# A token loop of graph layers on one core: layer 0 at both ends of the tensor phase, pair-0 results of layer 1 in evicted banks, new engine orders, one pair halved once

## The chip, the cores and the metric

One core of a Trainium2 chip runs the whole kernel. The metric is the time of one execution on the device in microseconds (us).

## What is computed

The reference has three parts. The first, the tokeniser, is the one that the change touches: for each of 64 × 64 frames (V = 75 nodes, 3 channels) it applies three graph layers and averages over the nodes.

```python
def _layer(x, A, W, b, g, be, m, v, relu):
    x = jnp.einsum('btvc,co->btvo', x, W)
    x = jnp.einsum('uv,btvo->btuo', A, x)
    x = x + b
    x = (x - m) * (g * jax.lax.rsqrt(v + EPS)) + be
    if relu:
        x = jax.nn.relu(x)
    return x
x = _layer(x, A, W0, b0, g0, be0, m0, v0, relu=True)     # 3 -> 128
x = _layer(x, A, W1, b1, g1, be1, m1, v1, relu=True)     # 128 -> 128
x = _layer(x, A, W2, b2, g2, be2, m2, v2, relu=False)    # 128 -> 64
return x.mean(axis=2)
```

The tokens are then joined with a text input, go through one attention layer and through 30 feed-forward steps (tanh, sigmoid gate, layer norm, 64 × 64 product). Those parts are the same in both kernels.

## The kernel before

`setup` folds the norms into the weights, splits weights into an fp16 high and an fp16 low part, and stores the input, already mixed by A once, in DRAM rows. `tokenise` (L478) is the token loop. `fuse` does the third layer's product, attention and feed-forward.

`tokenise` goes over GROUPS = 205 bodies. One body handles four sets of five frames; the sets are numbered in pairs, pair 0 and pair 1 (the argument p). A set has 5 × 75 = 375 columns. The stages of one pair are:

- layer 0 (`layer0`, L552, matmul L563): six matmuls of 64 rows into the PSUM banks 0 and 1. All pairs share these two banks.
- high and low parts of its ReLU: ScalarE writes the fp16 high part of bank 0, the f32 value of bank 0 and the fp16 high part of bank 1 (`y0_high`, L624 to L626). GpSimd makes the low part of the first (`y0_low`, L649), VectorE that of the second, straight from bank 1 (`y0_low`, L682). When L625 and L682 are done, the banks are free.
- mixing with A (`mix`, L567, matmul L580): 36 matmuls, two row halves side by side, into banks 2 and 3 for pair 0 and 4 and 5 for pair 1, one bank for each set of the pair.
- ScalarE takes the mixed result out of PSUM: fp16 high of the first set (`z1_high`, L630), f32 of the second (L631). VectorE makes the fp16 low part of the first (`z1_low`, L687).
- layer 1 (`layer1`, L586): three fp16 matmuls (L593 to L595) for the first set into bank 6, one f32 matmul (L599, two instructions) for the second into bank 7, for either pair.
- weighing (`weigh`, L693) on VectorE: ReLU against the bias and product with the column means of A, from bank 6 or 7 into `y1`. After that bank is free.
- pooling: GpSimd adds the nodes 0 to 36 onto 37 to 73 (`halve`, L658), then 37 to 55 onto 56 to 74 (L660), so that 19 numbers are left for a frame; VectorE sums these for both pairs at once (`pool_nodes`, L700), two bodies later.

All tiles between the stages exist twice (`par`), PSUM banks do not.

The order of the work is written out by hand, one list for each engine (`body` in each block), and kept together by counting semaphores: an engine waits until another's counter has reached a value. `y0_unit` and `pair_unit` turn body and pair into counts; in layer 0 pair 1 comes before pair 0, everywhere else pair 0 first. `steps` (L514) runs three bodies, a loop whose turn holds two bodies, and two last bodies. TensorE's body is: layer 0 of pair 1 of the next body, mixing of pair 0 and of pair 1, layer 0 of pair 0 of the next body, layer 1 of pair 1 of the body before, layer 1 of pair 0 of this one. SyncE fetches the input of the body after next once this body's layer 0 has been counted twice.

Of the kernel before, what the change touches and what calls it, by code (L numbers as in the profile page):

```python
# [36 lines left out]
GF = 5  # L37
# [440 lines left out]
def tokenise(nc, ps, zs, zst, z_stored, zst_loaded, pooledT, AThi, ATlo, abar, W0K, W1hi, W1lo, W1s, negb1):  # L478

    with ExitStack() as ctx:  # L480
# [29 lines left out]
        Y0B, Z1B, Y1B = 0, 2, 6  # L510
# [17 lines left out]
        def y0_unit(it, p):  # L528

            return it * PAIRS + 1 - p  # L530

        def pair_unit(it, p):

            return it * PAIRS + p

        with nc.Block() as block:
# [14 lines left out]
            def _(pe):  # L551
                def layer0(it, par, p, loads):  # L552

                    n = y0_unit(it, p)
                    if late(n, 1):
                        pe.wait_ge(y0f_done, n)
                        pe.wait_ge(y0lo_by_dve, n)
                    pe.wait_ge(zst_loaded[par], loads * (2 * 16))
                    for t in range(CHUNKS // 2):
                        for half in range(2):  # L560
                            rows = slice(HALF * half, HALF * half + HALF)
                            c0 = p * HC + t * C
                            last = nc.tensor.matmul(ps[:, Y0B + half, t * C:(t + 1) * C], zst[rows, par, c0:c0 + C],  # L563
                                                    W0K[rows, :], start=True, stop=True, skip_group_check=True)
                    last.then_inc(y0_ready, 1)

                def mix(it, par, p):  # L567

                    n = pair_unit(it, p)
                    pe.wait_ge(y0lo_by_pool, y0_unit(it, p) + 1)  # L570
                    pe.wait_ge(y0lo_by_dve, y0_unit(it, p) + 1)
                    if late(n, 2):
                        pe.wait_ge(z1lo_done, n - 1)
                        pe.wait_ge(z1f_done, n - 1)
                    for t in range(CHUNKS):
                        f0, w = SPAN[t]
                        for y, a in ((y0hi, AThi), (y0hi, ATlo), (y0lo, AThi)):
                            for j in range(2):
                                rows = slice(HALF * j, HALF * j + HALF)
                                last = nc.tensor.matmul(ps[:, Z1B + 2 * p + j, f0 * V:f0 * V + w],  # L580
                                                        y[rows, par, p, t * C:(t + 1) * C], a[rows, BAND0[t]:BAND0[t] + w],
                                                        start=(t == 0 and y is y0hi and a is AThi),
                                                        stop=(t == CHUNKS - 1 and y is y0lo), skip_group_check=True)
                    last.then_inc(z1_ready, 1)

                def layer1(it, par, p):  # L586

                    n = pair_unit(it, p)
                    pe.wait_ge(z1lo_done, n + 1)
                    if late(n, 1):  # L590
                        pe.wait_ge(y1_done[0], n)
                    o = ps[:, Y1B, 0:GV]
                    nc.tensor.matmul(o, W1hi[:], z1hi[:, par, p, :], start=True, stop=False)  # L593
                    nc.tensor.matmul(o, W1hi[:], z1lo[:, par, p, :], start=False, stop=False)
                    nc.tensor.matmul(o, W1lo[:], z1hi[:, par, p, :], start=False, stop=True).then_inc(y1_ready[0], 1)  # L595
                    pe.wait_ge(z1f_done, n + 1)
                    if late(n, 1):
                        pe.wait_ge(y1_done[1], n)
                    nc.tensor.matmul(ps[:, Y1B + 1, 0:GV], W1s[:], z1f[:, par, p, :], start=True, stop=True).then_inc(y1_ready[1], 1)  # L599

                layer0(0, 0, 1, 1)
                layer0(0, 0, 0, 1)

                def body(it, par, pair, last=False):

                    if not last:
                        layer0(it + 1, 1 - par, 1, pair + 2)
                    mix(it, par, 0)
                    mix(it, par, 1)
                    if not last:  # L610
                        layer0(it + 1, 1 - par, 0, pair + 2)
# [7 lines left out]
            def _(act):  # L619
                def y0_high(it, par, p):  # L620
                    act.wait_ge(y0_ready, y0_unit(it, p) + 1)
                    if late(it, 1):
                        act.wait_ge(y0lo_by_pool, y0_unit(it, p) - 1)
# [4 lines left out]
                def z1_high(it, par, p):  # L628
                    act.wait_ge(z1_ready, pair_unit(it, p) + 1)
                    nc.scalar.activation(z1hi[:, par, p, :], ps[:, Z1B + 2 * p, 0:GV], ACT.Identity).then_inc(z1hi_done, 1)  # L630
                    nc.scalar.activation(z1f[:, par, p, :], ps[:, Z1B + 2 * p + 1, 0:GV], ACT.Identity).then_inc(z1f_done, 1)  # L631

                y0_high(0, 0, 1)
                y0_high(0, 0, 0)

                def body(it, par, pair, last=False):
                    if not last:
                        y0_high(it + 1, 1 - par, 1)
                    z1_high(it, par, 0)
                    if not last:  # L640
                        y0_high(it + 1, 1 - par, 0)
                    z1_high(it, par, 1)
# [3 lines left out]
            def _(pool):  # L646
                def y0_low(it, par, p):
                    pool.wait_ge(y0f_done, y0_unit(it, p) + 1)
# [3 lines left out]
                def halve(it, par, p):  # L652

                    n = pair_unit(it, p)
# [4 lines left out]
                    pool.wait_ge(halved, n + 1)  # L659
                    nc.gpsimd.tensor_tensor(y[:, :, U2:V], y[:, :, U2:V], y[:, :, U1:U2], ALU.add).then_inc(quartered, 1)  # L660

                y0_low(0, 0, 1)
                y0_low(0, 0, 0)

                def body(it, par, pair, last=False):
                    if not last:
                        y0_low(it + 1, 1 - par, 1)
                    if late(it, 1):
                        halve(it - 1, 1 - par, 0)
                    if not last:  # L670
                        y0_low(it + 1, 1 - par, 0)
# [7 lines left out]
            def _(dve):  # L679
                def y0_low(it, par, p):  # L680
                    dve.wait_ge(y0hi_done, y0_unit(it, p) * 2 + 2)
# [3 lines left out]
                def z1_low(it, par, p):  # L685
                    dve.wait_ge(z1hi_done, pair_unit(it, p) + 1)
# [3 lines left out]
                def weigh(it, par, p, i):  # L690

                    dve.wait_ge(y1_ready[i], pair_unit(it, p) + 1)
                    nc.vector.scalar_tensor_tensor(y1[:, par, 2 * p + i].rearrange("p f v -> p (f v)"), ps[:, Y1B + i, 0:GV],  # L693
# [3 lines left out]
                def pool_nodes(it, par):  # L697

                    dve.wait_ge(quartered, it * PAIRS + PAIRS)
                    nc.vector.tensor_reduce(pooledT[:, :, bass.ds(it * GF, GF)], y1[:, par, :, :, U2:V], AX_X,  # L700
                                            ALU.add).then_inc(pooled, 1)

                y0_low(0, 0, 1)
                y0_low(0, 0, 0)

                def body(it, par, pair, last=False):
                    if late(it, 1):
                        weigh(it - 1, 1 - par, 0, 1)
                    if late(it, 2):
                        pool_nodes(it - 2, par)  # L710
                    if not last:
                        y0_low(it + 1, 1 - par, 1)
                    z1_low(it, par, 0)
                    if late(it, 1):
                        weigh(it - 1, 1 - par, 1, 0)
                        weigh(it - 1, 1 - par, 1, 1)
                    if not last:
                        y0_low(it + 1, 1 - par, 0)
                    z1_low(it, par, 1)
                    weigh(it, par, 0, 0)  # L720
                steps(dve, body)
                weigh(LAST, 0, 0, 1)
                pool_nodes(LAST - 1, 1)
                weigh(LAST, 0, 1, 0)
                weigh(LAST, 0, 1, 1)
                pool_nodes(LAST, 0)
# [669 lines left out]
```

## Time and profile before

| | |
|---|---|
| runs, median | 1706.89 us (1706.45 to 1708.33, 3 runs) |
| profiled execution, its own time | 1707.45 us |
| its span (first to last instruction) | 1705.5 us |
| TensorE (PE) busy | 1586.6 us, 93% |
| VectorE (DVE) busy | 1409.0 us, 83% |
| GpSimd (POOL) busy | 1344.2 us, 79% |
| ScalarE (ACT) busy | 1167.0 us, 68% |
| mean granted clock of TensorE | 0.98 |

The profile is one execution. PE is TensorE's matmuls, PEld its weight loads, which overlap them, PEldq the instructions that its queue handles itself (waits, registers). Matmuls are pipelined, so the time of one matmul is longer than the step to the next. An engine's step to its next instruction is shorter than the instruction for the same reason. Times of the rows are microseconds from the start of the span unless marked ns.

### The profile page before, as it was taken

How to read it: one execution, taken by the hardware profiler on the slowest of the kernel's cores; microseconds unless marked ns; L12 is line 12 of the kernel's file. 1: busy time of each engine (PE TensorE's matmuls, PEld its weight loads, DVE VectorE, ACT ScalarE, POOL GpSimd, SP SyncE). 2: the span in 40 equal slices, each digit the busy share in tenths (PEclk: the TensorE clock that was granted, in tenths of full speed). 3: DMA queues.
4: the chain of work that ended last, by engine and by line, in shares of the span. 5: the costliest groups of instructions: out<-in, count | busy, mean ns of one | idle time of the engine just before them, and what ended most of it. 6: DMA issues, size and time to landing. Idle time of an engine off the chain costs nothing. (4 is left out here: it accounts for less than half of the span.)

```text
span 1705.5 us, 65032 instructions
## 1 busy us (share of the span) xinstructions
PE 1586.6 (93%) x22590; PEld 1130.4 (66%) x22621; DVE 1409.0 (83%) x3355; ACT 1167.0 (68%) x2706; POOL 1344.2 (79%) x1496
## 2 busy tenths in 40 slices
PE   8599999999999999999999999999776899999999
PEld 8466666666666666666666666666565588888887
DVE  7388888888888888888888888888766799999998
ACT  3477777777777777777777777777243487887886
POOL 2388888888888888888888888888444688888887
PEclk9999999999999999999999999999788799999999
DMA  5200000000000000000000000000001000000001
GB/s 118 83 7 6 7 7 6 7 7 6 7 7 6 7 7 6 7 7 6 7 7 6 7 7 6 7 7 6 19 21 53 1 0 0 0 0 0 0 0 37
DMA packets 21666, 21.62 MB, mean 13 GB/s; under 512 B 12254, under 2 KB 19342, under 8 KB 21271
## 3 DMA queue, kind: packets, MB, share of 16 engines
q1 hardware_dynamic: 18554, 19.07, 4.1%
q0 software_dynamic: 1120, 1.44, 0.3%
q10 hardware_dynamic: 1972, 0.86, 0.2%
q8 instruction: 11, 0.18, 0.0%
q14 instruction: 9, 0.07, 0.0%
HBM read 14.43 MB, written 6.92 MB: 13 GB/s over the span
## 5 line engine op out<-in xcount | busy, mean ns | idle before, releaser
L693 DVE SCALAR_TENSOR_TENSOR y<-ps,negb,abar 128x375 f32<-128x375 f32 x820 | 477.7, 603 | 129.3 <-PE ps L595 124.8
L649 POOL TENSOR_TENSOR y0lo<-y_whole,y0hi 128x384 f16<-128x384 f32 x410 | 374.6, 914 | 144.9 <-ACT y_whole L625 132.0
L580 PE MATMUL ps<-AThi,y0hi 64*128 64x150 f16 (+1 forms) x4920 | 435.6, 217 | 5.7 <-POOL y0lo L649 3.6
L580 PE MATMUL ps<-AThi,y0lo 64*128 64x150 f16 (+1 forms) x4920 | 436.3, 215 | 0.0
L580 PE MATMUL ps<-ATlo,y0hi 64*128 64x150 f16 (+1 forms) x4920 | 436.0, 215 | 0.0
L624 ACT ACTIVATE y0hi<-ps 128x384 f16<-128x384 f32 x410 | 201.0, 490 | 328.8 <-PE ps L563 324.9
L658 POOL TENSOR_TENSOR y<-y 128x370 f32<-128x370 f32 x410 | 398.4, 972 | 7.6 <-DVE y L693 1.8
L1239 POOL TENSOR_TENSOR rs<-var,expo 128x8 f32<-128x8 f32 x180 | 313.0, 1749 | 66.0 <-DVE var L1307 66.0
L599 PE MATMUL ps<-z_whole,W1s 128*128 128x375 f32 x820 | 340.7, 497 | 0.1
L682 DVE SCALAR_TENSOR_TENSOR y0lo<-ps,y0hi 128x384 f16<-128x384 f32 x410 | 226.5, 552 | 73.8 <-ACT y0hi L626 73.8
L580 PEld LDWEIGHTS ps<-AThi,y0hi 64*128 64x128 f16 x4920 | 256.9, 94 | 21.0 <-issue 11.2
L580 PEld LDWEIGHTS ps<-ATlo,y0hi 64*128 64x128 f16 x4920 | 260.7, 96 | 0.0
L580 PEld LDWEIGHTS ps<-AThi,y0lo 64*128 64x128 f16 x4920 | 257.7, 94 | 0.0
L660 POOL TENSOR_TENSOR y<-y 128x190 f32<-128x190 f32 x410 | 218.0, 532 | 32.1
L687 DVE TENSOR_TENSOR z1lo<-ps,z1hi 128x375 f16<-128x375 f32 x410 | 221.1, 539 | 1.9 <-ACT z1hi L630 1.9
L631 ACT ACTIVATE z_whole<-ps 128x375 f32<-128x375 f32 x410 | 211.0, 515 | 0.0
L630 ACT ACTIVATE z1hi<-ps 128x375 f16<-128x375 f32 x410 | 206.8, 504 | 3.8 <-PE ps L580 3.8
L626 ACT ACTIVATE y0hi<-ps 128x384 f16<-128x384 f32 x410 | 204.2, 498 | 0.0
L625 ACT ACTIVATE y_whole<-ps 128x384 f32<-128x384 f32 x410 | 198.9, 485 | 0.0
L1282 PEld LDWEIGHTS ps<-w,gT 128*128 128x128 f32 x1440 | 189.9, 192 | 7.4 <-issue 0.7
L1282 PE MATMUL ps<-w,gT 128*128 128x128 f32 x1440 | 190.4, 275 | 1.8 <-issue 0.2
L599 PEld LDWEIGHTS ps<-z_whole,W1s 128*128 128x128 f32 x820 | 132.5, 189 | 83.3 <-issue 70.2
(197 smaller groups left out, 2421.0 us busy)
## 6 DMA issues: line engine op xcount, KB each, us to landing
z_static<-z_rows SPq DMA_DIRECT2D x410, 18.0 KB
xs<-in_x_v SPq DMA_DIRECT2D x5, 720.7 KB, 9.4
z_rows<-zp SPq DMA_DIRECT2D x10, 240.0 KB
h_rows<-h SPq DMA_DIRECT2D x16, 96.0 KB, 1.8
h2r<-h_rows SPq DMA_DIRECT2D x6, 256.0 KB, 2.7
out<-h2r SPq DMA_DIRECT2D x6, 256.0 KB, 2.3
z_rows<-zp POOLq DMA_DIRECT2D x5, 240.0 KB, 3.3
h<-in_txt SPq DMA_DIRECT2D x1, 512.0 KB, 4.9
```

Of the source, the lines that this page charges most:

```text
L580: last = nc.tensor.matmul(ps[:, Z1B + 2 * p + j, f0 * V:f0 * V + w], y[rows, par, p, t * C:(t + 1) * C], a[rows, BAND0[t]:BAND0[t] + w], s ...
L599: nc.tensor.matmul(ps[:, Y1B + 1, 0:GV], W1s[:], z1f[:, par, p, :], start=True, stop=True).then_inc(y1_ready[1], 1)
L630: nc.scalar.activation(z1hi[:, par, p, :], ps[:, Z1B + 2 * p, 0:GV], ACT.Identity).then_inc(z1hi_done, 1)
L631: nc.scalar.activation(z1f[:, par, p, :], ps[:, Z1B + 2 * p + 1, 0:GV], ACT.Identity).then_inc(z1f_done, 1)
L649: nc.gpsimd.tensor_tensor(y0lo[:, par, p, 0:HC], y0f[:, p, :], y0hi[:, par, p, 0:HC], ALU.subtract).then_inc(y0lo_by_pool, 1)
L658: nc.gpsimd.tensor_tensor(y[:, :, U1:2 * U1], y[:, :, U1:2 * U1], y[:, :, 0:U1], ALU.add).then_inc(halved, 1)
L660: nc.gpsimd.tensor_tensor(y[:, :, U2:V], y[:, :, U2:V], y[:, :, U1:U2], ALU.add).then_inc(quartered, 1)
L682: nc.vector.scalar_tensor_tensor(y0lo[:, par, p, HC:2 * HC], ps[:, Y0B + 1, 0:HC], 0.0, y0hi[:, par, p, HC:2 * HC], ALU.max, ALU.subtract) ...
L687: nc.vector.tensor_tensor(z1lo[:, par, p, :], ps[:, Z1B + 2 * p, 0:GV], z1hi[:, par, p, :], ALU.subtract).then_inc(z1lo_done, 1)
L693: nc.vector.scalar_tensor_tensor(y1[:, par, 2 * p + i].rearrange("p f v -> p (f v)"), ps[:, Y1B + i, 0:GV], negb1[:, 0:1], abar[:].rearran ...
L1239: nc.gpsimd.tensor_tensor(rs[:, b, :], var[:, b, :], expo[:], ALU.pow).then_inc(rs_done, 1)
L1282: last = nc.tensor.matmul(ps[:, cn, j * P:(j + 1) * P], gT[:, b, j * P:(j + 1) * P], wf, start=False, stop=(j == CP - 1), skip_group_check ...
```

## The change

Layer 0 of pair 0 now comes first in TensorE's body and that of pair 1 after the mixing. The results of layer 1 of pair 0 go to banks 5 and 4, from which the mixed results of pair 1 have just been taken, and only pair 1 uses banks 6 and 7; the waits follow from this. ScalarE, GpSimd and VectorE have new orders. Pair 1 is halved once only, and its sum over nodes reads 38 numbers for a frame where it read 19; `pool_nodes` does the pairs one after the other.

```diff
@@ -507,7 +507,8 @@
         quartered = sem("quartered")
         pooled = sem("pooled")
 
-        Y0B, Z1B, Y1B = 0, 2, 6
+        Y0B, Z1B = 0, 2
+        Y1B = ((5, 4), (6, 7))
         LAST = GROUPS - 1
         U1, U2 = V // 2, V // 2 + (V - V // 2) // 2
 
@@ -525,11 +526,7 @@
 
             return not isinstance(n, int) or n >= k
 
-        def y0_unit(it, p):
-
-            return it * PAIRS + 1 - p
-
-        def pair_unit(it, p):
+        def unit(it, p):
 
             return it * PAIRS + p
 
@@ -551,7 +548,7 @@
             def _(pe):
                 def layer0(it, par, p, loads):
 
-                    n = y0_unit(it, p)
+                    n = unit(it, p)
                     if late(n, 1):
                         pe.wait_ge(y0f_done, n)
                         pe.wait_ge(y0lo_by_dve, n)
@@ -566,12 +563,16 @@
 
                 def mix(it, par, p):
 
-                    n = pair_unit(it, p)
-                    pe.wait_ge(y0lo_by_pool, y0_unit(it, p) + 1)
-                    pe.wait_ge(y0lo_by_dve, y0_unit(it, p) + 1)
-                    if late(n, 2):
-                        pe.wait_ge(z1lo_done, n - 1)
-                        pe.wait_ge(z1f_done, n - 1)
+                    n = unit(it, p)
+                    pe.wait_ge(y0lo_by_pool, n + 1)
+                    pe.wait_ge(y0lo_by_dve, n + 1)
+                    if late(it, 1):
+                        if p == 0:
+                            pe.wait_ge(z1lo_done, n - 1)
+                            pe.wait_ge(z1f_done, n - 1)
+                        else:
+                            for i in range(2):
+                                pe.wait_ge(y1_done[i], unit(it - 1, 0) + 1)
                     for t in range(CHUNKS):
                         f0, w = SPAN[t]
                         for y, a in ((y0hi, AThi), (y0hi, ATlo), (y0lo, AThi)):
@@ -585,30 +586,34 @@
 
                 def layer1(it, par, p):
 
-                    n = pair_unit(it, p)
+                    n = unit(it, p)
                     pe.wait_ge(z1lo_done, n + 1)
-                    if late(n, 1):
-                        pe.wait_ge(y1_done[0], n)
-                    o = ps[:, Y1B, 0:GV]
+                    if p == 0:
+                        pe.wait_ge(z1f_done, unit(it, 1) + 1)
+                    elif late(it, 1):
+                        pe.wait_ge(y1_done[0], n - 1)
+                    o = ps[:, Y1B[p][0], 0:GV]
                     nc.tensor.matmul(o, W1hi[:], z1hi[:, par, p, :], start=True, stop=False)
                     nc.tensor.matmul(o, W1hi[:], z1lo[:, par, p, :], start=False, stop=False)
                     nc.tensor.matmul(o, W1lo[:], z1hi[:, par, p, :], start=False, stop=True).then_inc(y1_ready[0], 1)
                     pe.wait_ge(z1f_done, n + 1)
-                    if late(n, 1):
-                        pe.wait_ge(y1_done[1], n)
-                    nc.tensor.matmul(ps[:, Y1B + 1, 0:GV], W1s[:], z1f[:, par, p, :], start=True, stop=True).then_inc(y1_ready[1], 1)
-
+                    if p == 0:
+                        pe.wait_ge(z1lo_done, unit(it, 1) + 1)
+                    elif late(it, 1):
+                        pe.wait_ge(y1_done[1], n - 1)
+                    nc.tensor.matmul(ps[:, Y1B[p][1], 0:GV], W1s[:], z1f[:, par, p, :], start=True, stop=True).then_inc(y1_ready[1], 1)
+
+                layer0(0, 0, 0, 1)
                 layer0(0, 0, 1, 1)
-                layer0(0, 0, 0, 1)
 
                 def body(it, par, pair, last=False):
 
                     if not last:
-                        layer0(it + 1, 1 - par, 1, pair + 2)
+                        layer0(it + 1, 1 - par, 0, pair + 2)
                     mix(it, par, 0)
                     mix(it, par, 1)
                     if not last:
-                        layer0(it + 1, 1 - par, 0, pair + 2)
+                        layer0(it + 1, 1 - par, 1, pair + 2)
                     if late(it, 1):
                         layer1(it - 1, 1 - par, 1)
                     layer1(it, par, 0)
@@ -618,57 +623,58 @@
             @block.scalar
             def _(act):
                 def y0_high(it, par, p):
-                    act.wait_ge(y0_ready, y0_unit(it, p) + 1)
+                    act.wait_ge(y0_ready, unit(it, p) + 1)
                     if late(it, 1):
-                        act.wait_ge(y0lo_by_pool, y0_unit(it, p) - 1)
+                        act.wait_ge(y0lo_by_pool, unit(it, p) - 1)
                     nc.scalar.activation(y0hi[:, par, p, 0:HC], ps[:, Y0B, 0:HC], ACT.Relu).then_inc(y0hi_done, 1)
                     nc.scalar.activation(y0f[:, p, :], ps[:, Y0B, 0:HC], ACT.Relu).then_inc(y0f_done, 1)
                     nc.scalar.activation(y0hi[:, par, p, HC:2 * HC], ps[:, Y0B + 1, 0:HC], ACT.Relu).then_inc(y0hi_done, 1)
 
                 def z1_high(it, par, p):
-                    act.wait_ge(z1_ready, pair_unit(it, p) + 1)
+                    act.wait_ge(z1_ready, unit(it, p) + 1)
                     nc.scalar.activation(z1hi[:, par, p, :], ps[:, Z1B + 2 * p, 0:GV], ACT.Identity).then_inc(z1hi_done, 1)
                     nc.scalar.activation(z1f[:, par, p, :], ps[:, Z1B + 2 * p + 1, 0:GV], ACT.Identity).then_inc(z1f_done, 1)
 
+                y0_high(0, 0, 0)
                 y0_high(0, 0, 1)
-                y0_high(0, 0, 0)
 
                 def body(it, par, pair, last=False):
                     if not last:
+                        y0_high(it + 1, 1 - par, 0)
+                    z1_high(it, par, 0)
+                    z1_high(it, par, 1)
+                    if not last:
                         y0_high(it + 1, 1 - par, 1)
-                    z1_high(it, par, 0)
-                    if not last:
-                        y0_high(it + 1, 1 - par, 0)
-                    z1_high(it, par, 1)
                 steps(act, body)
 
             @block.gpsimd
             def _(pool):
                 def y0_low(it, par, p):
-                    pool.wait_ge(y0f_done, y0_unit(it, p) + 1)
+                    pool.wait_ge(y0f_done, unit(it, p) + 1)
                     nc.gpsimd.tensor_tensor(y0lo[:, par, p, 0:HC], y0f[:, p, :], y0hi[:, par, p, 0:HC],
                                             ALU.subtract).then_inc(y0lo_by_pool, 1)
 
                 def halve(it, par, p):
 
-                    n = pair_unit(it, p)
+                    n = unit(it, p)
                     pool.wait_ge(y1_done[0], n + 1)
                     pool.wait_ge(y1_done[1], n + 1)
                     y = y1[:, par, 2 * p:2 * p + 2].rearrange("p q f v -> p (q f) v")
                     nc.gpsimd.tensor_tensor(y[:, :, U1:2 * U1], y[:, :, U1:2 * U1], y[:, :, 0:U1], ALU.add).then_inc(halved, 1)
-                    pool.wait_ge(halved, n + 1)
-                    nc.gpsimd.tensor_tensor(y[:, :, U2:V], y[:, :, U2:V], y[:, :, U1:U2], ALU.add).then_inc(quartered, 1)
-
+                    if p == 0:
+                        pool.wait_ge(halved, n + 1)
+                        nc.gpsimd.tensor_tensor(y[:, :, U2:V], y[:, :, U2:V], y[:, :, U1:U2], ALU.add).then_inc(quartered, 1)
+
+                y0_low(0, 0, 0)
                 y0_low(0, 0, 1)
-                y0_low(0, 0, 0)
 
                 def body(it, par, pair, last=False):
                     if not last:
-                        y0_low(it + 1, 1 - par, 1)
+                        y0_low(it + 1, 1 - par, 0)
                     if late(it, 1):
                         halve(it - 1, 1 - par, 0)
                     if not last:
-                        y0_low(it + 1, 1 - par, 0)
+                        y0_low(it + 1, 1 - par, 1)
                     if late(it, 1):
                         halve(it - 1, 1 - par, 1)
                 steps(pool, body)
@@ -678,51 +684,51 @@
             @block.vector
             def _(dve):
                 def y0_low(it, par, p):
-                    dve.wait_ge(y0hi_done, y0_unit(it, p) * 2 + 2)
+                    dve.wait_ge(y0hi_done, unit(it, p) * 2 + 2)
                     nc.vector.scalar_tensor_tensor(y0lo[:, par, p, HC:2 * HC], ps[:, Y0B + 1, 0:HC], 0.0,
                                                    y0hi[:, par, p, HC:2 * HC], ALU.max, ALU.subtract).then_inc(y0lo_by_dve, 1)
 
                 def z1_low(it, par, p):
-                    dve.wait_ge(z1hi_done, pair_unit(it, p) + 1)
+                    dve.wait_ge(z1hi_done, unit(it, p) + 1)
                     nc.vector.tensor_tensor(z1lo[:, par, p, :], ps[:, Z1B + 2 * p, 0:GV],
                                             z1hi[:, par, p, :], ALU.subtract).then_inc(z1lo_done, 1)
 
                 def weigh(it, par, p, i):
 
-                    dve.wait_ge(y1_ready[i], pair_unit(it, p) + 1)
-                    nc.vector.scalar_tensor_tensor(y1[:, par, 2 * p + i].rearrange("p f v -> p (f v)"), ps[:, Y1B + i, 0:GV],
+                    dve.wait_ge(y1_ready[i], unit(it, p) + 1)
+                    nc.vector.scalar_tensor_tensor(y1[:, par, 2 * p + i].rearrange("p f v -> p (f v)"), ps[:, Y1B[p][i], 0:GV],
                                                    negb1[:, 0:1], abar[:].rearrange("p f v -> p (f v)"),
                                                    ALU.max, ALU.mult).then_inc(y1_done[i], 1)
 
                 def pool_nodes(it, par):
 
-                    dve.wait_ge(quartered, it * PAIRS + PAIRS)
-                    nc.vector.tensor_reduce(pooledT[:, :, bass.ds(it * GF, GF)], y1[:, par, :, :, U2:V], AX_X,
+                    dve.wait_ge(quartered, it + 1)
+                    nc.vector.tensor_reduce(pooledT[:, 0:2, bass.ds(it * GF, GF)], y1[:, par, 0:2, :, U2:V], AX_X, ALU.add)
+                    dve.wait_ge(halved, it * PAIRS + PAIRS)
+                    nc.vector.tensor_reduce(pooledT[:, 2:4, bass.ds(it * GF, GF)], y1[:, par, 2:4, :, U1:V], AX_X,
                                             ALU.add).then_inc(pooled, 1)
 
+                y0_low(0, 0, 0)
                 y0_low(0, 0, 1)
-                y0_low(0, 0, 0)
 
                 def body(it, par, pair, last=False):
-                    if late(it, 1):
-                        weigh(it - 1, 1 - par, 0, 1)
                     if late(it, 2):
                         pool_nodes(it - 2, par)
                     if not last:
-                        y0_low(it + 1, 1 - par, 1)
+                        y0_low(it + 1, 1 - par, 0)
                     z1_low(it, par, 0)
+                    z1_low(it, par, 1)
                     if late(it, 1):
                         weigh(it - 1, 1 - par, 1, 0)
                         weigh(it - 1, 1 - par, 1, 1)
+                    weigh(it, par, 0, 0)
                     if not last:
-                        y0_low(it + 1, 1 - par, 0)
-                    z1_low(it, par, 1)
-                    weigh(it, par, 0, 0)
+                        y0_low(it + 1, 1 - par, 1)
+                    weigh(it, par, 0, 1)
                 steps(dve, body)
-                weigh(LAST, 0, 0, 1)
-                pool_nodes(LAST - 1, 1)
                 weigh(LAST, 0, 1, 0)
                 weigh(LAST, 0, 1, 1)
+                pool_nodes(LAST - 1, 1)
                 pool_nodes(LAST, 0)
```

## Rows read from the trace of the kernel before

**Rows 1.** Busy time by engine over the token loop: stretch, length, busy (instructions), clock.

```profile
74.80:1206.00 1131.20, 1090.47 (x19109) 712.26 (x19105) 944.73 (x1829) 817.09 (x2035) 964.61 (x1218) 1.00 0.02 7
```

**Rows 2.** Timeline of TensorE's matmuls over one body: start us, length us, what.

```profile
605.34 0.34 PE L563 MATMUL ps<-W0K,z_static 64*128 64x128 f16 x6
605.52 0.20 PE L580 MATMUL ps<-AThi,y0hi 64*128 64x75 f16 x2
...
607.75 0.34 PE L563 MATMUL ps<-W0K,z_static 64*128 64x128 f16 x6
608.02 0.33 PE L593 MATMUL ps<-z1hi,W1hi 128*128 128x375 f16 x1
...
608.35 0.32 PE L595 MATMUL ps<-z1hi,W1lo 128*128 128x375 f16 x1
608.51 0.79 PE L599 MATMUL ps<-z_whole,W1s 128*128 128x375 f32 x2
609.47 0.32 PE L593 MATMUL ps<-z1hi,W1hi 128*128 128x375 f16 x1 [0.16 <-DVE y L693]
...
610.10 0.87 PE L599 MATMUL ps<-z_whole,W1s 128*128 128x375 f32 x2
610.90 0.34 PE L563 MATMUL ps<-W0K,z_static 64*128 64x128 f16 x6
```

**Rows 3.** Timeline of VectorE around the same body.

```profile
603.78 0.61 DVE L693 SCALAR_TENSOR_TENSOR y<-ps,negb,abar 128x375 f32<-128x375 f32 x1
604.31 0.55 DVE L682 SCALAR_TENSOR_TENSOR y0lo<-ps,y0hi 128x384 f16<-128x384 f32 x1
604.77 0.54 DVE L687 TENSOR_TENSOR z1lo<-ps,z1hi 128x375 f16<-128x375 f32 x1
...
605.22 1.12 DVE L693 SCALAR_TENSOR_TENSOR y<-ps,negb,abar 128x375 f32<-128x375 f32 x2
606.26 0.55 DVE L700 TENSOR_REDUCE pooledT<-y 128x380 f32 x1
607.09 0.56 DVE L682 SCALAR_TENSOR_TENSOR y0lo<-ps,y0hi 128x384 f16<-128x384 f32 x1 [0.28 <-ACT y0hi L626]
```

**Rows 4.** Timeline of TensorE's matmuls, the body before, after the loop's branch.

```profile
599.77 0.34 PE L563 MATMUL ps<-W0K,z_static 64*128 64x128 f16 x6
600.16 0.21 PE L580 MATMUL ps<-AThi,y0hi 64*128 64x75 f16 x2
...
602.18 0.35 PE L563 MATMUL ps<-W0K,z_static 64*128 64x128 f16 x6
```

**Rows 5.** Lines L557 and L558, instructions of TensorE's queue, 610 to 611 us.

```profile
L557 PEldq EVENT_SEMAPHORE  x1: 51/51/51, 610.6 to 610.6; - x1
...
L558 PEldq FUSED_REGOPS  x1: 37/37/37, 610.7 to 610.7; - x1
```

**Rows 6.** Timeline of TensorE, ScalarE and VectorE in the last body, without layer 0.

```profile
1205.87 0.21 PE L580 MATMUL ps<-AThi,y0hi 64*128 64x75 f16 x2
...
1207.10 0.48 ACT L630 ACTIVATE z1hi<-ps 128x375 f16<-128x375 f32 x1 [2.00 <-PE ps L580]
...
1208.11 0.48 ACT L630 ACTIVATE z1hi<-ps 128x375 f16<-128x375 f32 x1 [0.15 <-PE ps L580]
...
1207.62 0.55 DVE L687 TENSOR_TENSOR z1lo<-ps,z1hi 128x375 f16<-128x375 f32 x1 [0.29 <-ACT z1hi L630]
```

**Rows 7.** Timeline of ScalarE: the start of y0_high and what follows it.

```profile
605.80 0.49 ACT L624 ACTIVATE y0hi<-ps 128x384 f16<-128x384 f32 x1 [1.23 <-PE ps L563]
...
606.93 0.51 ACT L630 ACTIVATE z1hi<-ps 128x375 f16<-128x375 f32 x1
```

**Rows 8.** Groups by line: the second halving, GpSimd.

```profile
L660 POOL TENSOR_TENSOR y<-y 128x190 f32<-128x190 f32 x410 | 218.0, 532 | 32.1
```

**Rows 9.** TensorE after the loop: its first matmul there, and the stage.

```profile
1215.90 0.34 PE L891 MATMUL ps<-W2s,pooledT 128*64 128x64 f32 x1 [3.29 <-PEq L536]
...
1216.00:1344.00 128.00, 85.84 (x643) 67.53 (x645) 78.67 (x265) 39.65 (x97) 49.25 (x59) 0.74 0.13 31
```

## The prediction

> **What bounds the kernel now.** I read the stages first. The token loop fills 1131 of the 1705.5 us, with TensorE busy 1090 us of it at the full granted clock [rows 1]. The loop has 205 bodies, so nearly all of any gain or loss is a per-body number times some 203 (the first and the last body differ). Next I read TensorE through one body [rows 2]. Layer 0 of pair 1 starts at 605.34 and its successor at 610.90, so a body is 5.56 us. Three places in it are not matmul work. Layer 0 of pair 0 starts at 607.75: VectorE's pass that empties the layer-0 banks ends at 607.09 + 0.56 = 607.65 [rows 3], and TensorE follows 0.10 later. The second layer 1 starts at 609.47 though the first could have let go at 608.51 + 0.80 = 609.31 (0.80 is the step from 610.10 to 610.90): it waits for VectorE's weighing of bank 6, 0.16 us. Its f32 matmul starts at 610.10 and not 609.47 + 0.49 = 609.96 (0.49 is 608.02 to 608.51): it waits for the second weighing, 0.14 us. So TensorE sets the pace, with VectorE close behind: two banks for layer 0 and two for layer 1, each emptied by VectorE in order.
>
> **The change, part by part.** Times below are from the start T of the moment at which VectorE ends the pass that frees the layer-0 banks, since this is where I expect TensorE to stand and wait.
>
> *Layer 1 of pair 0 into banks 5 and 4.* This takes away the two waits above, 0.16 + 0.14 = 0.30 us per body. It adds waits for both pair-1 results of the mixing to be out of PSUM, which matters below.
>
> *VectorE's new order.* Before, one emptying pass (L682) stood behind pool_nodes, the other behind the two weighings of the body before, ahead of the second z1_low. Now the second one stands behind z1_low of both pairs and three weighings. That makes a ring in which every link is a true wait or the order of one engine: layer 0 of pair 0, mixing of pair 0, mixing of pair 1, z1_high of pair 1 on ScalarE, z1_low of pair 1, three weighings, y0_low of pair 1, and layer 0 of pair 0 again, which needs those banks. Its links:
>
> From T to the first matmul of layer 0: 0.10 (above). From there to the first matmul of the mixing: two rows differ. Where TensorE's sequencer is ahead it is 605.52 − 605.34 = 0.18 [rows 2]; where the sequencer was held up by the loop's branch, it is 600.16 − 599.77 = 0.39 [rows 4]. In the new kernel TensorE stands before layer 0, its sequencer has no lead, and the waits of the mixing are processed after the release, so I take 0.39. Queue instructions also lie between a passed wait and layer 0: in one body the wait starts at 610.6, lasts 51 ns, and layer 0 begins at 610.90, behind two register instructions [rows 2, 5]. That is 0.2 there; in the other body the wait is directly ahead of the load, but one more instruction follows it. I take 0.11 as the mean, with ends 0 and 0.2. Entry in all: 0.10 + 0.39 + 0.11 = 0.60, with bounds 0.28 and 0.69.
>
> The Trainium skill ("TensorE: Matmul & The Clock Gate", the table at its head) says that TensorE's queue is 64 deep and pulls weight loads ahead of matmuls in flight. By that rule the weight loads of the mixing would lie ready and the entry would be its lower bound; the gap of [rows 4] lies where no data was late, so here the trace does not bear the rule out for a queue that holds waits.
>
> From the first matmul of the mixing to z1_high of pair 1: in the last body, where nothing else holds ScalarE, 1208.11 − 1205.87 = 2.24 [rows 6]. z1_high itself 0.50 (0.48 and 0.51 [rows 6, 7]), and 0.04 to VectorE (1207.10 + 0.48 to 1207.62) [rows 6]. z1_low to the first weighing: 605.22 − 604.77 = 0.45. Weighing to weighing: twice 1.12 − 0.61 = 0.51. Third weighing to y0_low: 604.31 − 603.78 = 0.53. y0_low: 0.55 [rows 3]. Sum: 0.60 + 2.24 + 0.50 + 0.04 + 0.45 + 1.02 + 0.53 + 0.55 = **5.93 us**, against 5.56.
>
> *Does anything else end later within that ring?* TensorE: entry 0.60, two mixings 2.02 (600.16 to 602.18 [rows 4]) give 2.62 for layer 0 of pair 1 (its banks are free earlier: layer 0 to layer 0 took 607.75 − 605.34 = 2.41, from 0.10 on, so 2.51), 0.27 to layer 1, 1.29 for the first call, 0.65 to the end of the third fp16 matmul of the second (608.02 to 608.35 + 0.32), 0.04 on: 4.87, and VectorE reaches the third weighing at 3.38 + 0.45 + 1.02 = 4.85. That is a tie; I add nothing, and the rival "both late" prices it. ScalarE: y0_high of pair 1 would start after 2.84 + 0.76 and end 1.13 + 0.13 later (605.80 to 606.93 is three steps; the last instruction, 0.51 long at a step of 0.38, runs on for 0.13) [rows 7], at 4.86, ahead of 5.38 where y0_low wants it. It is covered.
>
> *Layer 0 at both ends.* Pair 0 first, pair 1 second, where it was the other way round: same six matmuls, same counts; the fetch of the next body's input waits for the same count of layer-0 results, at the same point of the body. Nothing, by symmetry.
>
> *The mixing of pair 1* now waits for two weighings of the body before. The last of them is behind y0_low and ends 0.53 − 0.06 + 0.61, about 1.1 us, after y0_low's start, so 0.5 after T; the mixing of pair 1 starts at 0.60 + 1.01. Covered by about 1 us.
>
> *Pooling.* GpSimd drops the second halving for pair 1, 532 ns [rows 8], and had idle time already: it worked 965 of 1131 us [rows 1]. Nothing in the loop. VectorE's one reduction (0.55 for 380 elements [rows 3]) becomes two, of 190 and 380. The added one is between 0 and 0.55. They stand after the last weighing and before y0_low of pair 0, whose input comes at about T + 1.8. From T + 0.4 on that leaves 1.4 for at most 1.1. Covered by 0.3. If that cover were gone, y0_low of pair 0 would be late and layer 0 of pair 1 with it, which has 0.1 us to spare (2.51 against 2.62).
>
> *The tail.* The last halving chain loses its second step, −0.5 us once.
>
> Sum: (5.93 − 5.56) × 203 = 75 us, less 0.5. The profiled execution took 1707.45 us (span 1705.5), 0.6 above the median of the three runs. On the median that gives 1706.9 + 74.6 = 1781.5. The entry leans to the low side of its bounds for bodies in which the queue instructions overlap the matmuls, so I say **1780**.
>
> **The rivals.**
>
> *Faster, the change does what its banks suggest.* If y0_low of pair 1 came before TensorE has run out of work, a body would be 5.56 − 0.30 = 5.26, and the time 1706.9 − 61 − 0.5 = 1645. For: both waits are really there [rows 2]. Against: VectorE's links alone put the release at 5.93. It decides where y0_low ends: before about 5.2 us into the body TensorE wins, after it VectorE does. 5 in 100.
>
> *No lost lead.* The sequencer gets through its waits unseen, entry 0.28, body 5.61, +10 − 0.5: 1716. For: 0.18 in one body of two. Against: in that body the wait ends at about 604.9 (604.31 + 0.55), 0.44 ahead of layer 0 [rows 2, 3], a lead that the new order removes. 8 in 100. This is what the skill's rule on the queue, cited above, would give.
>
> *Both late.* The tie at the third weighing goes against the ring: layer 1 has more waits in TensorE's queue, each some 0.1 us of it [rows 5]; three of them unhidden and the entry at its upper bound make the body 5.93 + 0.09 + 0.10 = 6.12, +113: 1820. 13 in 100.
>
> *The clock.* TensorE would stand about 0.7 us before layer 0 in each body. The granted clock fell to 0.74 on average in the stage after the loop, where TensorE was busy 86 of 128 us [rows 9]; if it fell to 1.2 GHz in the loop, the mixing's 2.24 would nearly double and the time pass 2000. Against: the loop would still have it busy near 85 of 100, and the stall just after the loop, 3.3 us, is over four times as long [rows 9]. 4 in 100.
>
> The forecast's own case has 70 in 100.
>
> **How the numbers follow.** The bounds of the entry give 5.61 to 6.02, 1716 to 1799. The range is 1730 to 1817: it takes in most of the forecast's case and most of "both late", and leaves out the lowest case, the faster one and the clock. A measurement of this kernel can tell 0.2% (3.4 us) from no change. Faster 0.05; same 0.03 (the lowest case, if its entry were hidden too); slower 0.92.
>
> **What the profile would show.** Right: layer 0 to layer 0 of the same pair 5.9 us; in TensorE's waits the load of L563 for the layer-0 banks, about 0.7 us each body, ended by VectorE's y0_low; no wait of layer 1 on the weighing; mixing 0.4 to 0.5 us after layer 0 in every body; VectorE without idle time from z1_low of pair 1 to y0_low of pair 1. Wrong: a body under 5.6, TensorE without that wait, or the third weighing waiting for TensorE.

## The result and the profile after

The changed kernel takes 1771.39 us (median of 4 runs, 1770.13 to 1773.23) against 1707.61 us for the kernel before in the same comparison: a ratio of 1.0374, 95% interval 1.0356 to 1.0392. It is slower by 64 us; forecast were 1780 us and slower, with a range of 1730 to 1817. The spans of the two profiled executions differ by 1768.0 − 1705.5 = 62.5 us.

Busy time by engine over the token loop of the changed kernel, with the columns of [rows 1]:

```profile
74.80:1265.00 1190.20, 1020.63 (x18993) 732.79 (x18993) 971.78 (x2021) 822.42 (x2024) 851.97 (x1011) 1.00 0.02 6
```

The loop is longer by about 60 us, all of the difference. The same matmuls show as 1021 us busy where [rows 1] has 1090, so that figure is not their work alone; GpSimd works 852 us for 965. The granted clock stayed full. What grew is the wait. Who waited for whom between 100 and 1200 us, in total, times, longest:

```profile
ACT y0hi L629 <- PE ps L560: 316.5, 187, 1.8
POOL y0lo L654 <- ACT y_whole L630: 297.3, 374, 1.2
PEld ps L560 <- issue: 252.8, 187, 1.4
...
PE ps L560 <- DVE y0lo L688: 76.7, 94, 0.8
PE ps L560 <- issue: 67.2, 93, 0.7
```

L560 is layer 0. TensorE stands before it for 76.7 + 67.2 us, in 187 bodies about 0.77 us each. In half of them the view names VectorE's y0_low (L688), in the other half "issue". There it is the same wait: an instruction of layer 0 in TensorE's queue (L555) waits from 598.8 for 1.80 us, y0_low ends at 599.99 + 0.54 = 600.53, and layer 0 starts at 600.63. ScalarE's and GpSimd's waits are those behind the late layer 0. No layer 1 waits for a weighing any more. One turn of the loop, two bodies, in TensorE's matmuls (start us, length us, what):

```profile
600.63 0.34 PE L560 MATMUL ps<-W0K,z_static 64*128 64x128 f16 x6 [0.72 <-issue]
600.96 0.21 PE L581 MATMUL ps<-AThi,y0hi 64*128 64x75 f16 x2
...
603.32 0.33 PE L596 MATMUL ps<-z1hi,W1hi 128*128 128x375 f16 x1
...
604.44 0.32 PE L596 MATMUL ps<-z1hi,W1hi 128*128 128x375 f16 x1
...
604.76 0.32 PE L598 MATMUL ps<-z1hi,W1lo 128*128 128x375 f16 x1
604.92 0.79 PE L604 MATMUL ps<-z_whole,W1s 128*128 128x375 f32 x2
606.50 0.34 PE L560 MATMUL ps<-W0K,z_static 64*128 64x128 f16 x6 [0.79 <-DVE y0lo L688]
606.95 0.21 PE L581 MATMUL ps<-AThi,y0hi 64*128 64x75 f16 x2
...
612.36 0.34 PE L560 MATMUL ps<-W0K,z_static 64*128 64x128 f16 x6 [0.72 <-issue]
612.73 0.21 PE L581 MATMUL ps<-AThi,y0hi 64*128 64x75 f16 x2
```

Two bodies last from 600.63 to 612.36, 5.87 us each, where [rows 2] has 5.56. Layer 1's two calls now follow each other without a stop (604.44 − 603.32 = 1.12), and after them TensorE stands from 604.92 + 0.79 to 606.50. VectorE over the same stretch:

```profile
599.99 0.54 DVE L688 SCALAR_TENSOR_TENSOR y0lo<-ps,y0hi 128x384 f16<-128x384 f32 x1
...
602.38 0.56 DVE L688 SCALAR_TENSOR_TENSOR y0lo<-ps,y0hi 128x384 f16<-128x384 f32 x1 [0.62 <-ACT y0hi L631]
602.86 0.54 DVE L693 TENSOR_TENSOR z1lo<-ps,z1hi 128x375 f16<-128x375 f32 x1
603.71 0.55 DVE L693 TENSOR_TENSOR z1lo<-ps,z1hi 128x375 f16<-128x375 f32 x1 [0.31 <-ACT z1hi L635]
604.17 1.63 DVE L699 SCALAR_TENSOR_TENSOR y<-ps,negb,abar 128x375 f32<-128x375 f32 x3
605.72 0.55 DVE L688 SCALAR_TENSOR_TENSOR y0lo<-ps,y0hi 128x384 f16<-128x384 f32 x1
606.18 0.60 DVE L699 SCALAR_TENSOR_TENSOR y<-ps,negb,abar 128x375 f32<-128x375 f32 x1
606.70 0.34 DVE L706 TENSOR_REDUCE pooledT<-y 128x190 f32 x1
606.95 0.54 DVE L708 TENSOR_REDUCE pooledT<-y 128x380 f32 x1
608.25 0.56 DVE L688 SCALAR_TENSOR_TENSOR y0lo<-ps,y0hi 128x384 f16<-128x384 f32 x1 [0.76 <-ACT y0hi L631]
...
611.71 0.55 DVE L688 SCALAR_TENSOR_TENSOR y0lo<-ps,y0hi 128x384 f16<-128x384 f32 x1
```

From 603.71 to 606.27 it goes without idle time through z1_low of pair 1, three weighings and y0_low of pair 1, and TensorE follows. That is the ring of the forecast.

### The profile page after: what moved, and what is told of

It is laid out like the page before. It is cut to its first block and busy times, and to the rows that moved or that the text cites. A ratio compares the mean times of both kernels' runs of the same rounds, so it can differ in the third digit from the quotient of the medians.

```text
span 1768.0 us, 65363 instructions
## 1 busy us (share of the span) xinstructions
PE 1520.5 (86%) x22621; PEld 1152.6 (65%) x22621; DVE 1441.5 (82%) x3560; ACT 1177.5 (67%) x2706; POOL 1235.1 (70%) x1291
## 5 line engine op out<-in xcount | busy, mean ns | idle before, releaser
L699 DVE SCALAR_TENSOR_TENSOR y<-ps,negb,abar 128x375 f32<-128x375 f32 x820 | 456.8, 599 | 0.6 <-PE ps L598 0.6
L629 ACT ACTIVATE y0hi<-ps 128x384 f16<-128x384 f32 x410 | 203.4, 496 | 358.3 <-PE ps L560 354.1
L688 DVE SCALAR_TENSOR_TENSOR y0lo<-ps,y0hi 128x384 f16<-128x384 f32 x410 | 226.6, 553 | 156.7 <-ACT y0hi L631 156.7
L604 PE MATMUL ps<-z_whole,W1s 128*128 128x375 f32 x820 | 325.3, 478 | 0.0
L581 PEld LDWEIGHTS ps<-AThi,y0hi 64*128 64x128 f16 x4920 | 277.6, 93 | 46.1 <-issue 36.3
L560 PE MATMUL ps<-W0K,z_static 64*128 64x128 f16 x2460 | 142.2, 218 | 171.3 <-DVE y0lo L688 81.6
L581 PEld LDWEIGHTS ps<-ATlo,y0hi 64*128 64x128 f16 x4920 | 280.1, 96 | 0.0
L581 PEld LDWEIGHTS ps<-AThi,y0lo 64*128 64x128 f16 x4920 | 279.5, 94 | 0.0
L560 PEld LDWEIGHTS ps<-W0K,z_static 64*128 64x128 f16 x2460 | 80.0, 94 | 290.2 <-issue 290.2
L631 ACT ACTIVATE y0hi<-ps 128x384 f16<-128x384 f32 x410 | 210.5, 513 | 0.0
L630 ACT ACTIVATE y_whole<-ps 128x384 f32<-128x384 f32 x410 | 205.0, 500 | 0.0
L636 ACT ACTIVATE z_whole<-ps 128x375 f32<-128x375 f32 x410 | 199.9, 487 | 0.0
```

The lines of the kernel that those rows point to most:

```text
L604: nc.tensor.matmul(ps[:, Y1B[p][1], 0:GV], W1s[:], z1f[:, par, p, :], start=True, stop=True).then_inc(y1_ready[1], 1)
L630: nc.scalar.activation(y0f[:, p, :], ps[:, Y0B, 0:HC], ACT.Relu).then_inc(y0f_done, 1)
L631: nc.scalar.activation(y0hi[:, par, p, HC:2 * HC], ps[:, Y0B + 1, 0:HC], ACT.Relu).then_inc(y0hi_done, 1)
L688: nc.vector.scalar_tensor_tensor(y0lo[:, par, p, HC:2 * HC], ps[:, Y0B + 1, 0:HC], 0.0, y0hi[:, par, p, HC:2 * HC], ALU.max, ALU.subtract) ...
```

## The experiments

All ran in rounds beside the kernel before, whose medians there were 1708.5 and 1708.6 us. In the diffs, `...` marks lines left out.

**1. The ring: y0_low of pair 1 one place earlier.**

```diff
-                    weigh(it, par, 0, 0)
                     if not last:
                         y0_low(it + 1, 1 - par, 1)
+                    weigh(it, par, 0, 0)
                     weigh(it, par, 0, 1)
```

> The changed kernel with VectorE's y0_low of pair 1 moved ahead of the third weighing. Theory (the ring through VectorE's order sets the body): y0_low of pair 1 can start when ScalarE is done, at about 605.23 where it started at 605.72 in the changed kernel's trace, so a body goes from 5.87 to about 5.38 us and the time from 1771 to about 1672 us. TensorE still waits for y0_low, but only 0.2 to 0.3 us. Rival (the body is held by something else, such as the longer way into the mixing or the two reductions): the time stays at 1771, or falls by less than 20 us.

Measured: 1674.48 us, ratio 0.9802 (0.9786 to 0.9819). Two steps swapped in VectorE's list turn 64 us lost into 34 us won. The timeline of this kernel's VectorE:

```profile
603.78 0.55 DVE L693 TENSOR_TENSOR z1lo<-ps,z1hi 128x375 f16<-128x375 f32 x1 [0.31 <-ACT z1hi L635]
604.25 1.12 DVE L699 SCALAR_TENSOR_TENSOR y<-ps,negb,abar 128x375 f32<-128x375 f32 x2
605.31 0.56 DVE L688 SCALAR_TENSOR_TENSOR y0lo<-ps,y0hi 128x384 f16<-128x384 f32 x1
605.78 1.11 DVE L699 SCALAR_TENSOR_TENSOR y<-ps,negb,abar 128x375 f32<-128x375 f32 x2
```

And of its TensorE:

```profile
600.72 0.34 PE L560 MATMUL ps<-W0K,z_static 64*128 64x128 f16 x6 [0.24 <-issue]
...
605.00 0.79 PE L604 MATMUL ps<-z_whole,W1s 128*128 128x375 f32 x2
606.11 0.34 PE L560 MATMUL ps<-W0K,z_static 64*128 64x128 f16 x6 [0.32 <-DVE y0lo L688]
...
611.48 0.34 PE L560 MATMUL ps<-W0K,z_static 64*128 64x128 f16 x6 [0.24 <-issue]
```

The pass that empties the banks, y0_low, ends at 605.87, and the body is 5.38 us (600.72 to 611.48 for two), the figure expected. The weighing that stood on the ring has moved off it and costs nothing there. The gain of 0.49 us a body is a little less than the weighing's step of 0.52: ScalarE's last instruction of y0_high, which y0_low needs, ends at 605.28 (604.75 + 0.53), only 0.03 before y0_low starts.

**2. The entry: the mixing without implied waits.**

```diff
...
-                    pe.wait_ge(y0lo_by_dve, n + 1)
+                    if last:
+                        pe.wait_ge(y0lo_by_dve, n + 1)
                     if late(it, 1):
-                        if p == 0:
-                            pe.wait_ge(z1lo_done, n - 1)
-                            pe.wait_ge(z1f_done, n - 1)
-                        else:
+                        if p == 1:
...
```

> The changed kernel without three waits of the mixing on TensorE that earlier waits of the same engine already imply (y0lo_by_dve for both pairs, z1lo_done and z1f_done for pair 0). Theory (instructions of TensorE's queue between the release and the mixing lie on the ring): the first matmul of the mixing follows VectorE's y0_low after 0.3 to 0.4 us where it was 0.47 and 0.68 in the two bodies of a turn, 0.2 to 0.3 us less per body, so 1711 to 1731 us. Rival (the entry is the array's own start after a pause): unchanged, 1771 within 4 us.

Measured: 1748.92 us, ratio 1.0237 (1.0219 to 1.0255): 22 us less than the changed kernel, where 40 to 60 less were expected. Both the theory's range (1711 to 1731) and the rival's (1771 within 4) missed it. The entry, the way from the end of y0_low to the first matmul of the mixing, did what the theory says, by this kernel's TensorE:

```profile
602.10 0.34 PE L560 MATMUL ps<-W0K,z_static 64*128 64x128 f16 x6 [0.62 <-issue]
602.27 0.21 PE L579 MATMUL ps<-AThi,y0hi 64*128 64x75 f16 x2
...
604.51 0.34 PE L560 MATMUL ps<-W0K,z_static 64*128 64x128 f16 x6
...
605.27 0.79 PE L602 MATMUL ps<-z_whole,W1s 128*128 128x375 f32 x2
```

The mixing follows layer 0 after 0.17 us in place of 0.33 to 0.45, so this gap is neither the array nor the data but the instructions in TensorE's queue. In the trace of after these are, between layer 0 at 600.63 and the mixing at 600.96, the waits of L568 and L572 (51 ns each) and a register instruction of L571 (32 ns), at 600.7, 600.9 and 600.8. With them the first weight load of the mixing starts at 600.93; here it starts at 602.21, while layer 0 still runs. The whole entry is 0.27 us in this body and 0.46 in the one after the loop's branch, for 0.43 and 0.68. What took half of these 0.2 us back is on VectorE:

```profile
605.02 0.55 DVE L691 TENSOR_TENSOR z1lo<-ps,z1hi 128x375 f16<-128x375 f32 x1 [0.15 <-ACT z1hi L633]
605.48 1.74 DVE L697 SCALAR_TENSOR_TENSOR y<-ps,negb,abar 128x375 f32<-128x375 f32 x3
607.14 0.55 DVE L686 SCALAR_TENSOR_TENSOR y0lo<-ps,y0hi 128x384 f16<-128x384 f32 x1
```

Three weighings take 1.74 us where they took 1.63: the second now waits for the f32 matmul of layer 1, which ends at 605.27 + 0.79 = 606.06, and starts at 606.10. With the mixing some 0.2 earlier, a second chain is as long as the ring: layer 0 of pair 0 at 602.10, the emptying of its banks, layer 0 of pair 1 at 604.51 (2.41 later, as in [rows 2]), layer 1.

**3. The pooling of before.** Both pairs halved twice, one reduction, in the changed kernel:

```diff
-                    if p == 0:
-                        pool.wait_ge(halved, n + 1)
-                        nc.gpsimd.tensor_tensor(y[:, :, U2:V], ...)
+                    pool.wait_ge(halved, n + 1)
+                    nc.gpsimd.tensor_tensor(y[:, :, U2:V], ...)
...
```

> The changed kernel with the pooling of before: both pairs halved twice by GpSimd, one reduction over both. Theory (pooling lies beside the ring on both engines): 1771 us within 4. Rival (the added reduction delays VectorE): about 0.26 us less per body, down to 1718 us.

Measured: 1770.06 us, against 1771.39. GpSimd is busy 959 us of the loop again and VectorE 33 us less, and nothing comes of either.

**4. One pair of banks.** Layer 1 of both pairs into banks 6 and 7, with the waits that this needs:

```diff
-        Y1B = ((5, 4), (6, 7))
+        Y1B = ((6, 7), (6, 7))
...
```

> The changed kernel with the results of both pairs in banks 6 and 7 again, as before. Theory (ring): layer 1 of pair 0 must wait for the first weighing, to about 604.91 where it started at 604.44, its third matmul ends at 605.55 and the third weighing starts 0.40 us later than now, inside the ring: 5.87 + 0.40 = 6.27 us a body, 1852 us. Rival (the new banks buy nothing since TensorE stands idle anyway): 1771 within 10 us.

Measured: 1857.36 us, ratio 1.0879 (1.0856 to 1.0902); expected were 1852. The third weighing now waits for TensorE, inside the ring, as this kernel's VectorE shows:

```profile
604.23 1.11 DVE L691 SCALAR_TENSOR_TENSOR y<-ps,negb,abar 128x375 f32<-128x375 f32 x2
605.66 0.61 DVE L691 SCALAR_TENSOR_TENSOR y<-ps,negb,abar 128x375 f32<-128x375 f32 x1 [0.31 <-PE ps L592]
606.18 0.55 DVE L680 SCALAR_TENSOR_TENSOR y0lo<-ps,y0hi 128x384 f16<-128x384 f32 x1
```

So the new banks are worth 86 us under the new orders, and the loss of the change as a whole is not theirs.

**5. A heavier reduction.**

```diff
-  nc.vector.tensor_reduce(pooledT[:, 0:2, ...], y1[:, par, 0:2, :, U2:V], AX_X, ALU.add)
+  nc.vector.tensor_reduce(pooledT[:, 0:2, ...], y1[:, par, 0:2, :, 0:V], AX_X, ALU.add)
```

> The changed kernel with VectorE's reduction of pair 0 over all 75 nodes of a frame where it reads the last 19, so that pair 0's pooled sum counts nodes more than once: 750 elements for 190. From 0.34 us for 190 and 0.54 for 380 it should take about 0.93, 0.59 more per body. Theory (the reductions stand in idle time of 0.62 and 0.76 us ahead of y0_low of pair 0, outside the ring): 1771 within 6 us. Rival (the cover is only 0.3 us, as the prediction had it, and what exceeds it pushes the ring): 1790 to 1830 us.

Measured: 1772.51 us. 0.58 us more work of VectorE in every body, 118 us in all, and the time is within the spread of the changed kernel's runs. Its VectorE:

```profile
601.52 0.92 DVE L706 TENSOR_REDUCE pooledT<-y 128x750 f32 x1
602.36 0.54 DVE L708 TENSOR_REDUCE pooledT<-y 128x380 f32 x1
602.93 0.56 DVE L688 SCALAR_TENSOR_TENSOR y0lo<-ps,y0hi 128x384 f16<-128x384 f32 x1
```

In the body shown this takes nearly all of the 0.62 us in which VectorE stood idle: y0_low of pair 0 (602.93) now follows the reductions directly. Compare experiment 1, where one weighing of 0.52 moved the time by 97 us: what counts is whether a VectorE instruction stands in the ring.

**6. The same waits taken out of the kernel before.** Its mixing loses `y0lo_by_dve` for both pairs, and `z1lo_done` and `z1f_done` for pair 0.

> The kernel before, without the waits of its mixing that earlier waits imply (y0lo_by_dve for both pairs, z1lo_done and z1f_done for pair 0). Theory (in the kernel before the late entry into the mixing is hidden, since layer 0 of pair 0 waits for the first emptying pass until 2.41 us anyway, and the mixings end at 2.2 to 2.4): unchanged, 1708 within 4 us. Rival (queue instructions cost the same wherever they stand): 0.1 us less per body, 1688 us.

Measured: 1708.81 us, ratio 1.0002 (0.9992 to 1.0011). The mixing does start 0.18 us after layer 0 in both bodies of a turn (600.44 to 600.62 and 606.00 to 606.18, where [rows 4] had 0.39), and nothing is gained: layer 0 of pair 0 still comes 2.41 us after that of pair 1 (600.44 to 602.85), held by the emptying of the banks. The same instructions cost nothing here and 22 us in the changed kernel.

**7. The banks alone, in the orders of before.** Only `Y1B`, the waits of `mix` and `layer1` and the bank in `weigh` are changed.

> The kernel before with the new banks and their waits alone, all orders as before. Theory (the new banks can only be used once both results of the mixing of pair 1 are out of PSUM, and the old orders have ScalarE end this at 610.13 and VectorE's second z1_low at 610.87 in the body shown, where the two matmuls of layer 1 start at 609.47 and 610.10): the f32 matmul starts 0.8 us later, 6.4 us a body, about 1870 us. Rival (the two waits of 0.30 us that go away are worth more): below 1700 us.

Measured: 1899.04 us, ratio 1.1113 (1.1089 to 1.1138), 29 us above the expectation. This kernel's TensorE:

```profile
602.61 0.79 PE L608 MATMUL ps<-z_whole,W1s 128*128 128x375 f32 x2
604.37 0.32 PE L600 MATMUL ps<-z1hi,W1hi 128*128 128x375 f16 x1 [0.97 <-ACT z_whole L640]
...
605.12 0.87 PE L608 MATMUL ps<-z_whole,W1s 128*128 128x375 f32 x2
605.92 0.34 PE L564 MATMUL ps<-W0K,z_static 64*128 64x128 f16 x6
```

The second layer 1 stands 0.97 us for the second instruction of ScalarE's z1_high of pair 1 (L640), which the old order has behind y0_high. The f32 matmul starts 2.51 us after the one of the call before, where [rows 2] has 1.59, so 0.92 and not 0.8 later. The new orders are what makes the banks usable.

**8. Both edits of experiments 1 and 2.**

> Both edits together: y0_low of pair 1 ahead of the third weighing, and the mixing without its implied waits. Theory (the entry into the mixing is on the ring until the next chain ties with it: layer 0 of pair 0, its emptying at 2.41 us, layer 1 of pair 1, the second weighing, y0_low): that next chain gives 2.41 + 0.28 + 1.28 + 0.04 + 0.52 + 0.55 + 0.1 to 0.3 = 5.2 to 5.3 us a body where the early y0_low alone has 5.38, so 1640 to 1660 us. Rival (the entry costs nothing once TensorE waits less): 1674 within 4 us.

Measured: **1644.15 us**, ratio 0.9617 (0.9599 to 0.9635) to the kernel before, the fastest of all. Its TensorE:

```profile
601.38 0.34 PE L560 MATMUL ps<-W0K,z_static 64*128 64x128 f16 x6 [0.24 <-DVE y0lo L686]
...
603.79 0.34 PE L560 MATMUL ps<-W0K,z_static 64*128 64x128 f16 x6
...
604.55 0.79 PE L602 MATMUL ps<-z_whole,W1s 128*128 128x375 f32 x2
...
605.66 0.79 PE L602 MATMUL ps<-z_whole,W1s 128*128 128x375 f32 x2
606.56 0.34 PE L560 MATMUL ps<-W0K,z_static 64*128 64x128 f16 x6
...
608.97 0.34 PE L560 MATMUL ps<-W0K,z_static 64*128 64x128 f16 x6
```

And its VectorE:

```profile
604.76 1.24 DVE L697 SCALAR_TENSOR_TENSOR y<-ps,negb,abar 128x375 f32<-128x375 f32 x2
605.91 0.55 DVE L686 SCALAR_TENSOR_TENSOR y0lo<-ps,y0hi 128x384 f16<-128x384 f32 x1
```

This body is 5.18 us (601.38 to 606.56), and the second chain of experiment 2 fills it: 2.41 from one layer 0 to the next, in which two banks are emptied, 1.55 to the end of layer 1's f32 matmul (605.34), 0.05 to the second weighing (605.39), 0.52 to y0_low, 0.55 for it, and 0.10 to layer 0. TensorE itself would be free at 605.66 + 0.80 = 606.46. The other body of the turn has the same chain, with 0.24 in place of 0.10 as the last step (layer 0 at 611.88), and is 5.32.

The kernels side by side:

| kernel | us |
|---|---|
| before | 1707.6 |
| changed | 1771.4 |
| changed, y0_low earlier | 1674.5 |
| changed, without the implied waits | 1748.9 |
| changed, pooling of before | 1770.1 |
| changed, one pair of banks | 1857.4 |
| changed, heavier reduction | 1772.5 |
| before, without the implied waits | 1708.8 |
| before, new banks alone | 1899.0 |
| changed, y0_low earlier and without the implied waits | 1644.2 |

## Why the prediction was right

**The ring.** Right, and shown by experiment 1 (a VectorE instruction taken out of it) with experiment 5 (more work of VectorE beside it). Its links by the trace of after: entry, from the end of y0_low to the mixing, 0.43, 0.68 and 0.47 us in the three bodies shown (600.53 to 600.96, 606.27 to 606.95, 612.26 to 612.73), 0.57 as the mean of the two kinds, for 0.60; from there to z1_high of pair 1, its length and the step to VectorE 2.75 (600.96 to 603.71) for 2.78; z1_low 0.46 for 0.45; two weighings 1.63 − 0.60 = 1.03 for 1.02; third weighing and y0_low 0.52 + 0.55 for 0.53 + 0.55. Together 5.88 for 5.93, and 5.87 measured over two bodies. Over what [rows 2] has, 0.31 × 203 = 63 us, for the 75 of the sum; the runs differ by 64.

**The term that was mis-sized** is the entry: 0.57 for 0.60, 6 us; the other links, 5.31 for 5.33, are 4 more. In the body after the loop's branch layer 0 follows y0_low's end by 0.23, in the other by 0.10. So the part put at 0.11 for queue instructions ahead of layer 0 is 0.13 in one body and nothing in the other, 0.07 in the mean. The mixing follows layer 0 by 0.45 in the one and by 0.33 to 0.37 in the other, 0.40 in the mean, for the 0.39 taken. It is the 0.11 that was too large. The prediction took 1.5 us off its sum of 1781.5 for this; 10 were due for all links together.

**The two waits that go away** did go: no row of layer 1 waiting for a weighing is left. Nothing was won by it against the kernel before, since TensorE then stands before layer 0. That is not to say that the old banks would have done: experiment 4 shows that under the new orders they cost 86 us more.

**"Faster"**, 1645 us, did not come: y0_low ends 5.6 us into the body (606.27 for a body that starts at 600.63), and the rival needed it before 5.2. Experiment 8 comes to 1644.15 us with y0_low moved up, but that the numbers agree is in part chance: TensorE's own matmuls are done 5.08 us into its body (601.38 to 606.46), not 5.26, and the second chain sets the pace.

**"No lost lead"**, 1716 us: refuted by the 0.33 to 0.45 us from layer 0 to the mixing, and by experiment 2, in which the waits' removal alone brings it to 0.17. The Trainium skill ("TensorE: Matmul & The Clock Gate", the table at its head) has the 64-deep queue pull weight loads ahead of matmuls in flight. In the trace of after the load behind the waits was not pulled ahead (it starts at 600.93, 0.03 before its matmul); in experiment 2, with these waits gone, it was (602.21, layer 0 running until 602.44).

**The tie at the third weighing** was taken too closely: 4.87 against 4.85. TensorE ends the third fp16 matmul at 604.76 + 0.32 = 605.08, and the weighing starts at 605.20 because VectorE comes from the one before; 0.08 us of slack after the 0.04 of the way. The step of 1.29 was read where an f32 matmul precedes layer 0, and between two calls of layer 1 it is 1.12. "Both late" lost its ground with that. The nearest chain meets VectorE at the second weighing, which the prediction did not look at: in the trace of after the f32 matmul before it ends at 603.81 + 0.79 = 604.60 and it starts at 604.69, a slack of 0.05 after the 0.04 of the way, and in experiment 2 it is the one that waits.

**Pooling** cost nothing, as said (experiment 3), but its cover is 0.62 and 0.76 us (the view of VectorE's idle time has these two before y0_low of pair 0) and not 0.3: the added reduction takes 0.34 us and its step is 0.26, half the upper bound.

**The tail's −0.5 us** can't be told from the spread of the runs, and no run has it alone. **The clock** stayed full in the loop.

## What to carry to other kernels

Where engines work through lists by hand, look for the ring: a wait of one engine, the orders of the others, and back. An instruction in it costs nearly its full step in every turn (0.49 of 0.52 us here), one beside it nothing as long as its idle time lasts, so that a swap of two lines (97 us here) can be worth more than the tiles they write. Before a wait is judged by the time it takes away, ask which resource is freed last after the change, and how many instructions the new order puts ahead of the one that frees it.

## What was not expected of the hardware

Waits that are already satisfied, with their register instructions, were not free on TensorE once it had no work queued: those between layer 0 and the mixing made 0.33 to 0.45 us of 0.17, and taking the implied ones out gave 22 us alone and 1674.5 − 1644.2 = 30 us on top of the other edit. In the kernel before, the same removal changed nothing (1708.81 us against 1708.57). There the mixing follows layer 0 after 0.18 us in one body [rows 2], with work still queued, and where it takes 0.39, the next layer 0 comes after 2.41 us all the same [rows 4].
